# Keys spread by a GpSimd multiplication, and value matmuls in four quarters of the array, in a four-layer gated cross-attention kernel

## What is computed

```python
def attend(q, k, v, bias, scale):              # per sequence, per head
    s = einsum('bhqd,bhkd->bhqk', q, k) * scale + bias
    return einsum('bhqk,bhkd->bhqd', softmax(s), v)

x = x + tanh(g_xattn[0]) * L0_xattn(layernorm(x), ctx)   # l0x: 16 heads of 64, 4 key heads, out through Wo
x = x + tanh(g_ffn[0])   * L0_ffn(layernorm(x))          # l0f: self attention, 16 heads of 8, plus 8 dense
                                                         #      experts weighted by a top-2 gate
x = x + tanh(g_xattn[1]) * L1_xattn(layernorm(x), ctx)   # l1x: 16 heads of 8, masked keys, out through Wo
x = x + tanh(g_ffn[1])   * L1_ffn(layernorm(x))          # l1f: shared + 7 gated SiLU experts
x = x + tanh(g_xattn[2]) * L2_xattn(layernorm(x), ctx)   # l2x: rotary, 4 heads of 32
x = x + tanh(g_ffn[2])   * L2_ffn(layernorm(x))          # l2f: one of 8 experts per token
x = x + tanh(g_xattn[3]) * L3_xattn(layernorm(x), ctx)   # l3x: 16 heads of 64, out through Wo
x = x + tanh(g_ffn[3])   * L3_ffn(layernorm(x))          # l3f: token-shift channel mix
```

## Time and profile before

| | us |
|---|---|
| median of 3 runs | 4558.1 (4556.83 to 4559.51) |
| profiled execution | 4552.95 |
| its span, first to last instruction | 4551.1 |
| PE busy in the span | 3947.3 (87%) |
| DVE busy | 3006.2 (66%) |
| ACT busy | 1735.9 (38%) |
| POOL busy | 764.9 (17%) |

### The profile page before, as it was taken

How to read it: one execution, slowest core, us unless ns; L and a number is a source line. 1 busy time by engine, 2 the same in 40 slices (tenths; PEclk the granted TensorE clock), 3 DMA queues, 4 the chain that set the end, 5 groups by cost and what they waited for, 6 DMA issues and landing times.

```text
span 4551.1 us, 105680 instructions
## 1 busy us (share of the span) xinstructions
PE 3947.3 (87%) x36890; PEld 3104.3 (68%) x36890; DVE 3006.2 (66%) x9082; ACT 1735.9 (38%) x4156; POOL 764.9 (17%) x575
## 2 busy tenths in 40 slices
PE   6999978888886888889999999777737899999965
PEld 4888855555554555589999999655537777777754
DVE  4666657777775777766666666799861355555569
ACT  3555534444442344333333333222203344444421
POOL 1222221111110000011111111100171122222211
PEclk9999987777776677689999999888758999999975
DMA  3000010000001000000000000100015200000000
GB/s 124 8 7 8 7 23 6 6 6 6 6 7 65 16 16 15 15 6 0 0 0 0 0 0 3 44 12 12 6 39 191 98 12 12 9 12 12 10 13 26
DMA packets 102053, 97.04 MB, mean 21 GB/s; under 512 B 31664, under 2 KB 91056, under 8 KB 101296
## 3 DMA queue, kind: packets, MB, share of 16 engines
q1 hardware_dynamic: 97408, 76.94, 5.6%
q0 software_dynamic: 4096, 8.40, 0.6%
q10 hardware_dynamic: 432, 10.19, 0.6%
HBM read 46.97 MB, written 19.66 MB: 15 GB/s over the span
## 4 chain that ended last, share of the span: by engine, by line
PE 60%; DVE 18%; SPq 8%; issue 7%; POOL 2%; DMA 2%; ACT 1%; DVEq 1%; POOLq 0%; ACTq 0%
PE ps L768 54%; SPq L591 7%; PE ps L936 5%; DVE acc L1658 2%; DMA arena_a<-kT 1%; DVE o_sb L1637 1%; POOL scr L718 1%; PE ps L806 1%; DVE arena_b L1606 1%; POOL route L740 1%; DVE xn L1442 1%; DVE x_sb L1557 1%; DVE st L1401 1%; DVE mx L1527 1%; DVE vsmall L1614 1%
## 5 line engine op out<-in xcount | busy, mean ns | idle before, releaser
L768 PE MATMUL ps<-xcT,small 128*128 128x256 f32 x2176 | 610.1, 419 | 34.7 <-DMA xcT<-in_ctxT 25.4
L732 POOL TENSOR_TENSOR rstd<-veps,neghalf 128x2 f32<-128x2 f32 (+1 forms) x224 | 167.9, 749 | 2403.8 <-DVE veps L1434 2071.2
L768 PEld LDWEIGHTS ps<-xcT,small 128*128 128x128 f32 x2176 | 411.3, 204 | 233.3 <-issue 114.5
L768 PE MATMUL ps<-arena_b,qT 64*64 64x64 f32 (+3 forms) x11136 | 541.8, 242 | 21.6 <-DVE arena_b L1606 20.3
L1278 ACT ACTIVATE kT<-ps 128x256 f32<-128x256 f32 (+1 forms) x768 | 294.4, 383 | 623.6 <-PE ps L768 547.4
L768 PE MATMUL ps<-small,xcT 128*64 128x64 f32 (+5 forms) x3072 | 482.7, 384 | 51.4 <-DVE acc L1658 30.3
L768 PE MATMUL ps<-xhi,parts_a 128*128 128x256 f32 (+1 forms) x2112 | 500.4, 289 | 22.7 <-DVE qT L1687 22.7
L768 PEld LDWEIGHTS ps<-arena_b,qT 64*64 64x64 f32 (+3 forms) x11136 | 463.5, 149 | 58.4 <-issue 35.0
L1248 ACT ACTIVATE pT<-ps 128x512 f32<-128x512 f32 (+1 forms) x576 | 303.3, 571 | 467.0 <-PE ps L936 465.3
L1687 DVE TENSOR_TENSOR qT<-kT,ps 128x256 f32<-128x256 f32 (+1 forms) x768 | 316.8, 419 | 188.5 <-ACT kT L1278 181.0
L768 PE MATMUL ps<-xlo,parts_a 128*128 128x256 f32 (+1 forms) x1536 | 430.6, 280 | 0.0
(11 more groups left out here) (212 smaller groups left out, 6388.5 us busy)
## 6 DMA issues: line engine op xcount, KB each, us to landing
wbuf<-parts_b SPq DMA_DIRECT2D x39, 512.0 KB, 3.0
arena_a<-kT SPq DMA_DIRECT2D x1024, 8.0 KB
xcT<-in_ctxT SPq DMA_DIRECT2D x96, 128.0 KB, 2.1
xn<-scr SPq DMA_DIRECT2D x39, 128.0 KB, 2.2
scr_y<-acc SPq DMA_DIRECT2D x39, 128.0 KB, 2.9
scr<-vsmall SPq DMA_DIRECT2D x9, 512.0 KB, 13.3
ctx_sb<-in_ctx SPq DMA_DIRECT2D x32, 128.0 KB, 2.1
arena_a<-in_w ACTq DMA_DIRECT2D x1, 4096.0 KB, 12.4
```

The lines of the kernel that those rows point to most:

```text
L732: pool.tensor_tensor(rstd[:, 0:n], veps[:, 0:n], neghalf[:, 0:n], ALU.pow).then_inc(s_rstd.sem, 1)
L768: return nc.tensor.matmul(o, lhsT, rhs, start=start, stop=stop, skip_group_check=True)
```

## The change

Two things are changed.

1. `k_spread` has 8 columns of heads in place of 16 (half as large). POOL writes it in one multiplication per group, kT repeated eight times by `own_head`, a table of 128 x 8 with a one where partition p belongs to head h (p // 8 mod 8). The table is made by DVE at the start from the identity. The 16 transfers per group, their semaphores and the clearing of the arena are gone. The scores read the same number of columns.
2. In l0x and l3x, the value matmuls run over (c, half, hb), so that the four 64x64 quarters take turns: for the second sequence of a tile (hb = 1) the output goes to the other half of the partitions of the bank. Number and width of the matmuls stay. ACT copies each bank in two ACTIVATEs of 64 partitions. For the second sequence the heads now stand the other way round in `oT`, so W does 16 matmuls of 128x64 with a copy of `Wo` whose halves are swapped, for hb = 1; that copy is loaded by two more transfers at the start (l0x) and in l2f (l3x).

```diff
@@ sync: the item QK
-                if item == ("QK", 0):
-                    sp.wait_ge(drained[layer.front_ring.bank(g, 1)], layer.front_ring.count(g, 1))
-                    for h in range(16):
-                        sp.dma_start(k_spread(g.par)[8 * h:8 * h + 8, h, :],
-                                     kT[8 * h:8 * h + 8, g.par, :]).then_inc(s_kspread.sem(g), 16)
@@ sync: at the start (l0x), and in l2f before load_tile(0) (l3x)
+                for half in range(2):
+                    sp.dma_start(wo_swapped[half * S:(half + 1) * S, :],
+                                 src[(1 - half) * S:(2 - half) * S, a:b]).then_inc(s_swap, 16)
@@ gpsimd
-                    pool.memset(arena_a[:, 0:4096], 0.0).then_inc(s_zero, 1)
+                    pool.wait_ge(s_heads, 2)
...
+                if item == ("QK", 0):
+                    pool.wait_ge(drained[layer.front_ring.bank(g, layer.use(item))],
+                                 layer.front_ring.count(g, layer.use(item)))
+                    pool.tensor_tensor(k_spread(g.par), kT[:, g.par, :].unsqueeze(1).to_broadcast([P, 8, GT]),
+                                       own_head[:, :].unsqueeze(2).to_broadcast([P, 8, GT]),
+                                       ALU.mult).then_inc(s_kspread.sem, 1)
@@ tensor: heads_times_values
-                blocks = [(0, hb) for hb in range(2)] if layer is L0X else [(i, hb) for i in range(4) for hb in range(2)]
-                for turn in ((0, 1), (1, 0)):
...
+                n = 2 if layer is L0X else 8
+                for c, half, hb in itertools.product(range(n), range(2), range(2)):
+                    rows = slice(half * S, (half + 1) * S)
+                    to = slice((half ^ hb) * S, ((half ^ hb) + 1) * S)
+                    w0, heads = 512 // n, 8 // n
+                    last = mm(bank(banks[half])[to, c * w0:(c + 1) * w0],
+                              v_heads(layer, g.par)[rows, 2 * t + hb, c, :],
+                              pT[rows, t, c * heads:(c + 1) * heads, hb * S:(hb + 1) * S])
+                    if (c, hb) == (n - 1, 1):
+                        last.then_inc(filled[banks[half]], 1)
@@ tensor: W
+                    if chunks == 8:
+                        for c in range(8):
+                            for hb in range(2):
+                                toks = slice(hb * S, (hb + 1) * S)
+                                wo = w(layer.name + "_wo") if hb == 0 else wo_swapped
+                                last = mm(bank(b)[toks, 0:D], oT[:, t, c, toks], wo[:, c * D:(c + 1) * D],
+                                          start=c == 0, stop=c == 7)
@@ scalar: A
-                        nc.scalar.activation(o, i, ACT.Copy).then_inc(drained[b], 1)
+                        for hb in range(2):
+                            rows = slice((j ^ hb) * S, ((j ^ hb) + 1) * S)
+                            last = nc.scalar.activation(oT[rows, t, :, hb * S:(hb + 1) * S],
+                                                        bank(b)[rows, :].rearrange("p (c q) -> p c q", q=S), ACT.Copy)
+                        last.then_inc(drained[b], 1)
@@ vector
-                    dve.memset(arena_a[:, 4096:8192], 0.0).then_inc(s_zero, 1)
```

More of the change, by code:

```diff
@@ L12 @@
+import itertools
 from contextlib import ExitStack
@@ L289, in build @@
         onemu = sb("onemu", [P, 2])
+        own_head = sb("own_head", [P, 8])
         bv_col = sb("bv_col", [P, 1])
@@ L347, in build @@
         s_ctx = dma_step("s_ctx", l0x=16, l1x=16, l2x=16, l3x=16)
-        s_kspread = dma_step("s_kspread", l0f=256, l1x=256)
+        s_kspread = step("s_kspread", l0f=1, l1x=1)
         s_rope = step("s_rope", l2x=4)
@@ L383, in build @@
         s_bv = ctx.enter_context(nc.semaphore("s_bv"))
+        s_heads = ctx.enter_context(nc.semaphore("s_heads"))
         s_ones = ctx.enter_context(nc.semaphore("s_ones"))
+        s_swap = ctx.enter_context(nc.semaphore("s_swap"))
         s_rest = ctx.enter_context(nc.semaphore("s_rest"))
@@ L527, in _ @@
                 sp.sem_inc(s.sem, s.credit)
-            for s in (s_ctx, s_kspread):
+            for s in (s_ctx,):
                 for i in range(2):
@@ L631, in experts @@
                 sp.wait_ge(s_lo, 16)
+                a = LATE.index("l3x_wo") * 1024
+                swap_wo(late_in, a, a + 1024)
                 load_tile(0)
@@ L772, in start @@
                     pe.wait_ge(s_small, 16)
+                    pe.wait_ge(s_swap, 32)
                     pe.wait_ge(s_const, 3)
@@ L783, in start @@
                     pe.wait_ge(s_late, 16)
+                    pe.wait_ge(s_swap, 64)
                     pe.wait_ge(m_out, TILES2)
@@ L860, in heads_times_values @@
                 pe.sem_inc(s_ready, 1)
-                blocks = [(0, hb) for hb in range(2)] if layer is L0X else [(i, hb) for i in range(4) for hb in range(2)]
-                for turn in ((0, 1), (1, 0)):
[L863 to L874, removed]
-                                          pT[rows, t, 4 * j + i, hb * S:(hb + 1) * S])
-                            if turn == (1, 0) and (i, hb) == blocks[-1]:
-                                last.then_inc(filled[banks[j]], 1)
+                n = 2 if layer is L0X else 8
[8 more added lines that the diff above has]
+                        last.then_inc(filled[banks[half]], 1)
             def do(layer, item, g):
@@ L897, in do @@
                         if layer in (L0F, L1X):
-                            pe.wait_ge(s_kspread.sem(g), s_kspread.all(g))
+                            pe.wait_ge(s_kspread.sem, s_kspread.after(g, 0))
                     if layer in (L0F, L1X):
@@ L905, in do @@
                                           qT[rows, g.par, 0, t * P + hb * S:t * P + (hb + 1) * S],
-                                          k_spread(g.par)[rows, 8 * half:8 * half + 8,
-                                                          t * P + hb * S:t * P + (hb + 1) * S])
+                                          k_spread(g.par)[rows, :, t * P + hb * S:t * P + (hb + 1) * S])
                     if layer is L2X:
@@ L1191, in do @@
                     b = wait_filled(fr, g, u)
-                    act.wait_ge(s_kspread.sem(g.back(2)), s_kspread.all(g.back(2)))
+                    act.wait_ge(s_kspread.sem, s_kspread.after(g.back(2), 0))
                     nc.scalar.activation(qT[:, g.par, 0, :], bank(b, GT), ACT.Identity,
@@ L1384, in start @@
                     dve.wait_ge(m_const, 3)
+                    dve.tensor_reduce(den[:, 0, 0:16], ident.rearrange("p (h d) -> p h d", d=8), AX_X,
+                                      ALU.add).then_inc(s_heads, 1)
+                    dve.wait_ge(s_heads, 1)
+                    dve.tensor_tensor(own_head[:, :], den[:, 0, 0:8], den[:, 0, 8:16], ALU.add).then_inc(s_heads, 1)
+                    dve.wait_ge(s_heads, 2)
             def statistics(layer, g):
```

21 lines of the change are left out of this document (8 added, 13 removed).

## The result

| | before | changed |
|---|---|---|
| median, us | 4558.2 (4556.83 to 4559.51) | 4633.3 (4631.69 to 4638.16) |
| ratio, with 95% interval | | 1.0168 (1.0152 to 1.0184) |
| profiled execution, us | 4552.95 | 4634.06 |

The change costs 75 us. To see where, every stage is measured from POOL's power of its first group (L732, in the changed kernel L739) to that of the next stage; there are 32 in a stage. "Period" is the mean distance of two of them in groups 8 to 28; the "last stretch" of a stage is the time from its last power to the first of the next stage.

A forecast was written before the change was run, and what follows sets the result against it. PE was taken to bound l0x and l3x, the order of dependences l0f and l1x. Terms -24 - 53 + 118 - 3.5 + 6 + 3 = +46.5 gave 4599.5 against 4552.95, 4605 on the median; range 4555 to 4672.

The forecast's parts named there:

- l0f, +118 forecast: l0f keys: routing starts 3.7 us later in each of 32 groups, nothing absorbs it; +118 us (bounds +54 and +125).
- queue step: l0f: GpSimd works in order, so a 3.80 us multiplication stands ahead of the two powers and delays DVE's routing by 3.7.
- the clock as a rival: l0f and l1x: PE's clock rises earlier, by up to 1.5 us a group, giving 4557, or later by as much; 8%.
- the exclusion it used in l1x: l1x: multiplication and DVE operations with two SBUF inputs exclude each other; second subtraction waits 1.4 us, 17.3 a group.
- l1x, +6 forecast: l1x keys: +10 for 0.35 us a group, 12 off for the first two transfer waits, +8 other order; bounds -33 and +75.
- The rival in which GpSimd gets in first: l1x: the first subtraction waits some 3.7 us, 19.7 a group; +72 in place of +6, whole 4671; 12%.
- 8 us more for groups in the other order: l1x: allowance of +8 us for a few groups where kT comes earlier and the multiplication starts ahead of DVE's first subtraction.
- l3x, -53 forecast: l3x value matmuls: each A saves 0.92 us, 1.64 a group over 32 groups; -53 us (bounds -30 and -59).
- The wait before A1: l3x: A0's evacuation ends at 4017.5, so A1, which could start at 4017.27, waits 0.25 us.
- l0x, -24: l0x value matmuls: A0's gain lost to evacuation, A1's 0.79 us kept, less 0.05 for W; -24 us (0 to -48).
- -3.5 for the clearing: Before l0f's first group: two clearings of 4096 columns go, one of them on the path; -3.5 us.
- the price that the forecast set on the swapped Wo: 0.5 MB more loaded ahead of the first context tile and l2f's first expert tile; +3 us (0 to 8).

The follow-up runs named there:

- experiment 3: Changed kernel, with l0f's GpSimd multiplication moved behind the gate's power instead of ahead of both powers; l1x left as is: 4598.2 us, ratio 1.0087.
- Experiment 5: Changed kernel, multiplication moved in both loops: in l0f until V is evacuated, in l1x behind DVE's first subtraction: 4496.6 us, ratio 0.9866.
- experiment 8: Changed kernel, but in l1x ACT spreads the keys with eight ACTIVATEs scaled by `own_head`, four behind each exponential: 4591.5 us, ratio 1.0077.
- experiment 4: Changed kernel with one 128-partition ACTIVATE per bank of A in l0x and l3x, in place of two; those outputs not the reference's: 4593.8 us, ratio 1.0073.
- 6: Changed kernel with l0x's transpose F of xn moved ahead of S1 and P0: 4625.3 us, ratio 1.0149.
- 10: Changed kernel with Wo's product in l0x and l3x again eight 128-column matmuls, unswapped Wo alone; those outputs not the reference's: 4634.5 us, ratio 1.0164.
- experiment 1: Changed kernel with the keys' part alone; value matmuls, W, Wo and evacuation as in the kernel before: 4676.3 us, ratio 1.0260.
- experiment 2: Kernel before with the values' part alone put in; sixteen transfers a group stay in l0f and l1x: 4522.3 us, ratio 0.9915.

## Why the prediction was right, and where it was off

The forecast was 4605 with 4555 to 4672, slower; measured 4633.3, slower. The forecast's mechanism held in the main, and the sum was 28 us short. Between the two profiled executions, from which the stages are read, the difference is 81 us and the sum 35 short. It came this near in part by luck: l1x was forecast 14 us too dear, and l0x and l3x together were credited 35 us too much. Step by step:

- **l0f, +118 forecast, +124.5 found.** The queue step is as described: kT, multiplication, two powers, routing. The multiplication was 3.60 and not 3.80 (the row of the same form, doubled, was 5% too dear), and the routing came 3.45 later. From one kT to the next a longer group grew by 3.60 and a shorter one by 3.50 (table of experiment 3): nothing absorbed it, as forecast. The mean period grew by 3.95, because in the kernel before every fourth group is a short one, in which T1 and the scores run at TensorE's upper level, and in the changed kernel only two of 27 are. These five groups, 2.5 us each, are some 12 of the 124; the forecast had the clock as a rival, at 1.5 us a group. That l0f came out 6 us over the forecast and not under it is owed to them. Experiment 5 gives all of it back.
- **What the prediction missed in l0f** is that the exclusion it used in l1x holds here too (L1551, 1.92). Where the multiplication stood it added nothing that can be seen: a group grew by the multiplication's own 3.60, since the powers behind it were later anyway. Experiment 3 shows it: with the queue free 3.2 of the 3.6 us a group stay, now by the exclusion. The two causes cover each other, and who removes only the one he sees gets a ninth (and 28 us of clock that came with it).
- **l1x, +6 forecast, -8.3 found.** The sum for the loop was right in kind: 15.9 without exclusion (15.73 in experiment 8) and 17.3 with it (17.07). The rival in which GpSimd gets in first isn't an alternative but every second group: 17.8 with it (forecast 19.7), 16.4 with the other order (forecast 17.3); the subtraction waits 2.7 and 0.9 where 3.7 and 1.4 were set. So the mean grew by 0.17 and not by 0.35 with 8 us more for groups in the other order: +5 in place of +18. The edges gave back 13 to 14, 12 were set: the first three distances of the stage were 3.0, 26.4 and 17.6 and are 8.9, 13.7 and 14.1, and the last stretch is 53.2 in place of 56.8.
- **l3x, -53 forecast, -34.6 found.** A's 0.92 twice is there, and W with its neighbours saves 0.07 where 0.05 was set. The wait before A1 was set at 0.25 and is 0.56: four ACTIVATEs take 2.28, not 2.1, and end 3.48 behind A0's start, not 3.25. That is the mis-sized term: 1.35 and not 1.64 a group, which over 32 groups would be -43. It holds in the steady groups only: from the second power to the last the stage is 38.9 shorter. And its edges grew: the first distance is 15.5 and the last stretch 60.6, in place of 14.6 and 57.1. With one evacuation a bank (experiment 4) the last stretch is 51.4; more of it wasn't taken apart.
- **l0x, -24 and -3.5 for the clearing forecast, -10.4 found.** From A0 to A1 it took 3.79 and takes 3.94. A0's gain is lost as forecast, but the first reason is another one: xcT, which ACT makes behind P0, keeps the query product waiting 0.63, and only then comes the evacuation with 0.29. From A1 to W0 0.76 is gained (forecast 0.79), W0 to V0 costs 0.23 where 0.05 was set, V0 to S0 gains 0.06: 0.44 a group, as the period. Experiments 4, 6 and 10 take the evacuation, xcT and W away one at a time and get 0.29, 0.27 and 0.27. From the third power to the last this is 12.6 us.
- **The edges of l0x.** The second distance of the stage takes 2 us back (33.1 in place of 31.2), about the price that the forecast set on the swapped Wo: it is 31.9 to 33.4 in all runs that load it at the start and 30.4 to 31.2 in the others. The clearing is worth what was forecast, but is paid away again: the last stretch is 68.8 before, 64.6 without the clearing (experiment 1), 72.9 with it and the values' part (experiment 2) and 69.0 in the changed kernel, so the clearing gives 4 and the values' part takes as much; with one evacuation a bank (experiment 4) it is 62.5. The forecast set nothing for a stage's end.
- **l1f, 0 forecast, +5.6 found**: not in any step; the place in SBUF. l2x and l2f have the same period and lie between 682 and 687 in all runs; with 685.1 in experiment 1, which loads no swapped Wo, the runs don't show a price for that load there.

The rules of the Trainium skill stand as follows. "SBUF — State Buffer", section Who interferes with whom, names the DVE operations that dispute GpSimd's port: two SBUF inputs, or a copy or tensor_scalar in a two-port mode, never a reduction or an instruction with one SBUF input outside such a mode. Every row here agrees for the multiplication: L1544, L1499, L1576 and L1551 are blocked, L1542 (reduction), L1539 and L1680 (a PSUM operand) aren't. In the changed kernel all 63 DVE instructions of the blocked kinds (L1544, L1489, L1551) that start inside one of the 64 multiplications are recorded longer, and none of the 85 others. It doesn't agree for the power: L1572 with two SBUF inputs takes 0.35 at 1079.50, inside L754. The 4.497 us for a 2048-wide add of two inputs that the prediction cites from the Trainium skill's "GPSIMD Engine Reference", section Performance versus the Vector engine, are more than this multiplication takes: 3.60.

## What to carry to other kernels

A GpSimd instruction has two prices beside its own time: what stands behind it in GpSimd's queue, and which DVE instructions with two SBUF operands fall inside it. Before placing it, list by name what DVE runs in the next few microseconds and take a stretch that reads PSUM or reduces; here the same 3.60 us cost 3.6 us in every group or nothing. And after a matmul gets cheaper, look in turn at each thing that was hidden under it: xcT, the evacuation and the tile shapes of W each took a share, and freeing one handed part of it to the next.

## What was not expected of the hardware

- 32 bytes more ahead of the weights in SBUF slow a dense stage of matmuls by 0.14 us in 29.2 (0.5%), at full clock; taken away again, the time comes back.
- An ACTIVATE of 64 partitions by 512 columns takes as long as one of 128 (four in 2.28, two in 1.09), as a 64x256 and a 128x256 did.
- A multiplication with both operands repeated by broadcast takes 3.60 us for 2048 columns, 5% less than twice the 1.90 of 1024 columns; beside a DVE instruction that got in first it shows as 4.53.
- A power on GpSimd doesn't block DVE's two-input instructions, a multiplication does.
